# Mixture of experts in a decoder kernel: features on partitions, static order, the expert's weights copied by two engines

## The reference, cut to what matters

```python
logits = x @ gate_w.T + gate_b
topk_logits, topk_idx = jax.lax.top_k(logits, K)          # K = 4
topk_weight = jax.nn.softmax(topk_logits, axis=-1)
xt, gid = xs[order], flat_idx[order]                      # token copies, sorted by expert
gate = jax.lax.ragged_dot(xt, w_gate, group_sizes) + b_gate[gid]
up = jax.lax.ragged_dot(xt, w_up, group_sizes) + b_up[gid]
gate = jnp.minimum(gate, 7.0)
up = jnp.clip(up, -7.0, 7.0)
activated = (up + 1.0) * gate * jax.nn.sigmoid(1.702 * gate)
outs = jax.lax.ragged_dot(activated, w_down, group_sizes) + b_down[gid]
y = jnp.sum(outs[inv].reshape(-1, K, Hh) * topk_weight[..., None], axis=1)
```

## Time and profile before

| | before |
|---|---|
| median of 3 runs | 1018.72 us (1017.98 to 1022.2) |
| the profiled execution's own time | 1018.88 us |
| its span | 1017.2 us |
| TensorE's mean granted clock | 0.884 |
| PE busy | 809.6 us, 80% |
| DVE, ACT, POOL busy | 749.9, 488.3, 459.5 us |
| blocks of experts, first PE instruction to last copy | from 456.15 to 595.2 us of the span |

### The profile page before, as it was taken

The page is one execution under the profiler, slowest core; times in us unless marked ns, Lnnn a source line. Parts: engine busy times, 40 slices in busy tenths (PEclk is TensorE's granted clock), DMA queues, the critical chain, the costliest instruction groups (busy, mean ns, idle before and its releaser), DMA issues. The chain is left out here.

```text
span 1017.2 us, 16391 instructions
## 1 busy us (share of the span) xinstructions
PE 809.6 (80%) x4620; PEld 608.5 (60%) x4624; DVE 749.9 (74%) x1562; ACT 488.3 (48%) x1262; POOL 459.5 (45%) x512
## 2 busy tenths in 40 slices
PE   6798999999799999429999933577799999980165
PEld 3477999997699998317777721224455555550133
DVE  2576777777688887585666635787799999959977
ACT  0233444444355555003333312258898878608185
POOL 1004444442455553536555537140588889813111
PEclk9879999999999999558999975788799999995577
DMA  8707000000400001003444435100333323110000
GB/s 291 245 1 319 14 0 0 0 0 1 174 2 0 0 0 36 6 13 108 125 128 124 124 125 188 60 0 4 124 103 104 99 87 104 42 42 0 0 11 32
DMA packets 29836, 72.06 MB, mean 71 GB/s; under 512 B 5362, under 2 KB 19314, under 8 KB 27298
## 3 DMA queue, kind: packets, MB, share of 16 engines
q1 hardware_dynamic: 25186, 58.95, 16.6%
q0 software_dynamic: 4608, 12.59, 4.7%
HBM read 60.97 MB, written 10.55 MB: 70 GB/s over the span
## 5 line engine op out<-in xcount | busy, mean ns | idle before, releaser
L1718 POOL TENSOR_TENSOR arena<-arena 128x1024 f32<-128x1024 f32 x63 | 147.6, 2371 | 30.7 <-DVE arena L1684 30.7
L1684 DVE TENSOR_TENSOR_SCAN arena<-arena,ps 128x1024 f32<-128x1024 f32 x64 | 143.5, 2275 | 13.6 <-PE ps L1605 8.5
L662 POOL TENSOR_TENSOR arena<-arena 128x256 f32<-128x256 f32 x64 | 46.6, 728 | 195.4 <-DVE arena L656 195.4
L1625 PE MATMUL ps<-arena 128*128 128x512 f32 x256 | 120.1, 592 | 0.0
L712 ACT ACTIVATE arena<-arena 128x128 f32<-128x128 f32 x256 | 98.9, 390 | 19.3 <-DVE arena L682 18.7
L721 ACT ACTIVATE arena<-ps 128x512 f32<-128x512 f32 x64 | 38.2, 598 | 131.4 <-PE ps L609 131.4
L589 PE MATMUL ps<-arena 128*128 (+3 forms) x768 | 96.8, 277 | 2.5 <-PEq L731 0.9
L589 PEld LDWEIGHTS ps<-arena 128*128 128x128 f32 (+1 forms) x768 | 91.5, 193 | 4.1 <-issue 2.9
L1650 ACT ACTIVATE arena<-arena 128x1016 f32<-128x1016 f32 x64 | 72.4, 1135 | 22.9 <-DVE arena L1684 22.8
L1660 ACT ACTIVATE arena<-arena 128x256 f32<-128x256 f32 x192 | 81.2, 494 | 0.1
L1060 POOL DMA_INDIRECT arena<-tokens,arena x64 | 64.0, 1000 | 28.8 <-issue 23.4
(11 more groups left out here) (319 smaller groups left out, 1786.0 us busy)
## 6 DMA issues: line engine op xcount, KB each, us to landing
arena<-c_rows SPq DMA_DIRECT2D x32, 512.0 KB, 3.7
arena<-in_E_gu SPq DMA_DIRECT2D x8, 1024.0 KB, 12.1
expert_out<-arena SPq DMA_DIRECT2D x64, 128.0 KB
arena<-in_E_dn SPq DMA_DIRECT2D x1, 4096.0 KB, 13.7
arena<-in_ctxT SPq DMA_DIRECT2D x2, 1024.0 KB, 5.2
arena<-in_X_o SPq DMA_DIRECT2D x1, 2048.0 KB, 19.9
arena<-in_A_o SPq DMA_DIRECT2D x1, 2048.0 KB, 27.2
arena<-in_F_w SPq DMA_DIRECT2D x2, 1024.0 KB
```

Source lines behind the costliest of these rows:

```text
L1625: t = eng.matmul(ps[:, 2 * k + half, :], ident, hC[s % 4][:, half * 512:(half + 1) * 512], start=False, stop=n == ST - 1)
L1684: eng.tensor_tensor_scan(hst[s % 4], dA[s % 4], psD[s % 2].rearrange("p k m -> p (k m)"), 0.0, ALU.mult, ALU.add).then_inc(h_ready, 1)
L1718: eng.tensor_tensor(hC[s % 4], hst[s % 4], Csb[i % 4], ALU.mult).then_inc(hC_ready, 1)
```

## The change

The steps keep features on partitions throughout, and every engine's order is written out without a loop.

- **Gate and up** (`gate_up`): the weights are now stationary and the turned tokens move. Output is features x tokens, so the activation comes out as the down product needs it: `TA`, `AT`, `actT` are gone. Four fp32 matmuls of 128 columns take the place of two of 256.
- **The weights** of a block must lie at a fixed address for this: `wcur`, two buffers. DVE copies the gate half (`weights`), ACT the up half (`up_weights`), 128x256 fp32 each, at an address from a register that each loads itself (`reg_load`). The copy of block s waits for gate and up of s-2.
- **Biases** of gate and up are now one value for each partition and are added by DVE in the operations that limit (`limits`), again at a register's address; both bias matmuls and `split3` are gone. The down bias, weighted by the gate weights, is added once at the end: before the blocks DVE spreads `gw` over the experts (`prod`, `spread`, operations of 128x1024), PE turns it (two transposes), ACT copies it to `weightT`; after the blocks PE makes eight products of 32 rows and 256 columns, and DVE adds them to `x` in four operations of 128x512 ahead of the combination.
- **Order.** PE: turn of s+2, gate and up of s+1, down of s-1. ACT: up weights of s+2, tokens of s+2, output copy of s-1 (which was DVE's `YO`), sigmoid of s+1. DVE: gate weights of s+2, limits of s+1, gated product of s. POOL gathers directly with `tok_i`, without the copy.
- One more small load (`E_bias_dn`) and a smaller `E_bias`.

```diff
-                    eng.tensor_copy(tok_u[:, v:v + 1], tok_i[:, bass.ds(s + 1, 1)]).then_inc(tok_ready, 1)
                     eng.indirect_dma_start(xin[:, u], None, hd,
-                                           bass.IndirectOffsetOnAxis(ap=tok_u[:, u:u + 1].bitcast(u32), axis=0)
+                                           bass.IndirectOffsetOnAxis(ap=tok_i[:, s:s + 1].bitcast(u32), axis=0)
                                            ).then_inc(x_in[u], 16)
...
-                    for c in range(DC):
-                        eng.matmul(ps[:, 2 + d, 0:2 * I], xinT[:, d, c, :],
-                                   wgu[:, c, bass.ds(e, 1), :].rearrange("p a m -> p (a m)"), start=c == 0, stop=False)
-                    eng.matmul(ps[:, 2 + d, 0:2 * I], sel[0:3 * E, bass.ds(e, 1), :].rearrange("p a m -> p (a m)"),
-                               bias_b[0:3 * E, 0:2 * I], start=False, stop=True).then_inc(gu_done, 1)
-
-                def TA(i, u):
...
-                    eng.transpose(ps[:, 4 + d, 0:P], act_[:, d], ident).then_inc(aT_done, 1)
...
+                def gate_up(s):
+                    d = s % 2
                     eng.wait_ge(xT_ready, s + 1)
+                    eng.wait_ge(wg_ready, s + 1)
+                    eng.wait_ge(wu_ready, s + 1)
+                    if s >= 2:
                         eng.wait_ge(up_ready, s - 1)
+                    for k in range(2):
+                        for c in range(DC):
+                            t = eng.matmul(ps[:, 2 + d, k * I:(k + 1) * I], wcur[:, d, c, k * I:(k + 1) * I],
+                                           xinT[:, d, c, :], start=c == 0, stop=c == DC - 1)
+                    t.then_inc(gu_done, 1)
...
+                def down(s):
...
                     eng.wait_ge(act_ready, s + 1)
...
+                    eng.matmul(ps[:, 6 + d, 0:D], act_[:, d], wdn[:, bass.ds(e, 1), :].rearrange("p a m -> p (a m)"),
+                               start=True, stop=True).then_inc(dn_done, 1)
...
+                for s in range(NBLK + 1):
+                    if s + 2 < NBLK:
+                        turn(s + 2)
+                    if s + 1 < NBLK:
+                        gate_up(s + 1)
+                    if s >= 1:
+                        down(s - 1)
+                    if s < NBLK:
+                        eng.reg_mov(e_down, e_next)
+                    if s + 1 < NBLK:
+                        eng.reg_load(e_next, owner_i[0:1, s + 1:s + 2])
...
+                def up_weights(s):
+                    eng.reg_load(e_a, owner_i[0:1, s:s + 1])
+                    if s >= 2:
+                        eng.wait_ge(gu_done, s - 1)
+                    e = eng.snap(e_a, min_val=0, max_val=E - 1)
+                    eng.activation(wcur[:, s % 2, :, I:2 * I],
+                                   wgu[:, :, bass.ds(e, 1), I:2 * I].rearrange("p c a m -> p c (a m)"),
+                                   ACT.Copy).then_inc(wu_ready, 1)
...
+                for s in range(NBLK + 1):
+                    if s + 2 < NBLK:
+                        up_weights(s + 2)
+                        tokens(s + 2)
+                    if s >= 1:
+                        rows(s - 1)
+                    if s + 1 < NBLK:
+                        sigmoid(s + 1)
...
+                def weights(s):
+                    eng.reg_load(e_w[s % 3], owner_i[0:1, s:s + 1])
+                    if s >= 2:
+                        eng.wait_ge(gu_done, s - 1)
+                    eng.tensor_copy(wcur[:, s % 2, :, 0:I],
+                                    wgu[:, :, bass.ds(owner_of(s), 1), 0:I].rearrange("p c a m -> p c (a m)")
+                                    ).then_inc(wg_ready, 1)
+
+                def limits(s):
...
+                    eng.tensor_scalar(gate[:, d], ps[:, 2 + d, 0:I], bias_gu[:, bass.ds(e, 1), 0], 7.0, ALU.add,
+                                      ALU.min).then_inc(gate_ready, 1)
+                    eng.tensor_scalar(up[:, d], ps[:, 2 + d, I:2 * I], bias_gu[:, bass.ds(e, 1), 1], 8.0, ALU.add,
+                                      ALU.min).then_inc(up_ready, 1)
...
+                for s in range(NBLK):
+                    if s + 2 < NBLK:
+                        weights(s + 2)
+                    if s + 1 < NBLK:
+                        limits(s + 1)
+                    gated(s)
...
+                for b in range(NB):
+                    rows = slice((b % 4) * E, (b % 4 + 1) * E)
+                    t = eng.matmul(ps[:, b, 0:D], weightT[rows, b // 4], bias_dn[rows],
+                                   start=True, stop=True)
...
+                for k in range(NB // 2):
+                    eng.wait_ge(bias_done, k + 1)
+                    two = x[:, 2 * k:2 * k + 2]
+                    ch.mark(eng.tensor_tensor(two, two, ps[:, 2 * k:2 * k + 2, 0:D], ALU.add))
+                ch.wait()
```

More of the change, by code:

```diff
@@ L818, in decoder @@
         sel = view(51104, 2048, "p (e m) -> p e m", dt=bf16, e=E)
-        bias_f = view(A0 + 10240, 512)
-        bias_b = view(A0 + 10752, 256, dt=bf16)
+        bias_gu = view(A0 + 10240, 2 * E, "p (e k) -> p e k", k=2)
+        bias_dn = view(A0 + 10304, D)
+        weightT = view(A0 + 10560, 256, "p (g t) -> p g t", g=2)
         def prefetch_down(eng):
             load(eng, "wdn", wdn, a["E_dn"])
-            load(eng, "bias", bias_f[0:3 * E, :], a["E_bias"])
+            load(eng, "bias", bias_gu, a["E_bias"])
+            load(eng, "bias_dn", bias_dn, a["E_bias_dn"])
             for b in range(NB):
@@ L1079, in _, with turn @@
             def _(eng):
[L1080 to L1085, removed]
+                def turn(s):
+                    d, u = s % 2, s % 4
+                    eng.wait_ge(x_in[u], 16 * (s // 4) + 16)
+                    if s >= 2:
                         eng.wait_ge(xT_ready, s - 1)
@@ new lines, in _ @@
+                loaded(eng, "wgu", "wdn")
+                eng.reg_load(e_next, owner_i[0:1, 0:1])
+                eng.wait_ge(spread_step, 2)
+                for g in range(2):
+                    t = eng.transpose(ps[:, 4, g * P:(g + 1) * P],
+                                      spread[:, 4 * g:4 * g + 4].rearrange("p b e -> p (b e)"), ident)
+                t.then_inc(wT_done, 1)
+                turn(0)
+                turn(1)
+                gate_up(0)
+                for s in range(NBLK + 1):
[9 more added lines that the diff above has]
+                        eng.reg_load(e_next, owner_i[0:1, s + 1:s + 2])
@@ L1141, in _, with tokens @@
             @block.scalar
             def _(eng):
-                def XT(i, u):
-                    s, d = 4 * i + u, u % 2
+                def tokens(s):
+                    d = s % 2
                     eng.wait_ge(xT_done, s + 1)
-                    if not early(i, 2, s):
+                    if s >= 2:
                         eng.wait_ge(gu_done, s - 1)
@@ L1149, in XT, with sigmoid @@
                                    ACT.Copy).then_inc(xT_ready, 1)
-                def SG(i, u):
-                    s, d = 4 * i + u, u % 2
+                def sigmoid(s):
+                    d = s % 2
                     eng.wait_ge(gate_ready, s + 1)
-                    if not early(i, 2, s):
+                    if s >= 2:
                         eng.wait_ge(gs_ready, s - 1)
                     eng.activation(sig[:, d], gate[:, d], ACT.Sigmoid, scale=1.702).then_inc(sig_ready, 1)
[L1158 to L1163, removed]
@@ L1165, in _, with rows @@
-                pipeline(eng, NBLK // 4, [(2, XT), (1, SG), (0, AT)], [(0, XT), (1, XT), (0, SG)], [])
+                def rows(s):
+                    u = s % 4
+                    eng.wait_ge(dn_done, s + 1)
+                    if s >= 4:
+                        eng.wait_ge(y_out[u], 16 * (s // 4))
+                    eng.activation(yout[:, u], ps[:, 6 + s % 2, 0:D], ACT.Copy).then_inc(y_ready, 1)
+                e_a = eng.alloc_register("e_a")
+                def up_weights(s):
+                    eng.reg_load(e_a, owner_i[0:1, s:s + 1])
+                    if s >= 2:
+                        eng.wait_ge(gu_done, s - 1)
[3 more added lines that the diff above has]
+                                   ACT.Copy).then_inc(wu_ready, 1)
@@ new lines, in _ @@
+                loaded(eng, "wgu")
+                up_weights(0)
+                eng.wait_ge(wT_done, 1)
+                eng.activation(weightT, ps[:, 4, 0:2 * P].rearrange("p (g t) -> p g t", g=2), ACT.Copy).then_inc(wT_ready, 1)
+                tokens(0)
+                up_weights(1)
+                tokens(1)
+                sigmoid(0)
+                for s in range(NBLK + 1):
[6 more added lines that the diff above has]
+                        sigmoid(s + 1)
@@ L1183, in GS, with gated @@
+                def gated(s):
+                    d = s % 2
                     eng.wait_ge(sig_ready, s + 1)
@@ L1185, in GS @@
                     eng.wait_ge(gs_ready, s + 1)
-                    if not early(i, 2, s):
```

(25 more changed lines are left out.)

96 lines of the change are left out of this document (27 added, 69 removed).

## The result

| | before | after |
|---|---|---|
| median | 1019.8 us (1017.98 to 1022.2, 4 runs) | 1002.45 us (1001.38 to 1006.94, 4 runs) |
| ratio | | 0.9834, 95% interval 0.9802 to 0.9867 |
| profiled execution, span | 1018.88, 1017.2 us | 1006.94, 1005.2 us |
| stage of the experts | 149.0 us | 131.5 us |
| one block, mean of 50 | 2.10 us | 1.82 us |

The change brings 17.4 us (1019.8 - 1002.45); 28.5 were forecast (27.5 in the blocks, 1.0 at the start).

The account below looks back on a forecast made before the run. PE was taken to bound the blocks: 2.10 us each falling to 1.67, over 64 blocks, saves 27.5 us; with 1.0 at the start, 1018.9 becomes 990.4 us. The range was 981 to 1007 us.

Parts of the forecast that it names:

- rival 1: ACT's queue becomes the bound through a ring over two blocks: 1.85 us a block, 1002 us; chance 0.22.
- PE's own steps: PE in each block: transposes 0.21, gate and up 0.90, down product 0.43, together 1.54 us without stalls.
- Rival 4: PE's four more weight loads a block aren't hidden, 0.19 each: 2.43 us a block, 1039 us; chance 0.03.
- The stalls: PE's late issue kept per block: 0.06 us ahead of the down product and 0.07 unplaced.
- The loop's cost: PE's sequencer late at the loop's turn: 0.085 and 0.05 us a block, both to go with the loop.
- The step that failed: DVE's work per block summed to 1.59 us with its register load overlapped, 1.88 exposed; 1.59 taken, under PE's 1.67.
- Adding the bias through a pointer I cost at nothing: DVE's limits: two register addresses of 0.055 us lie beside running operations, costing nothing; 0.11 if that cover fails.
- second form: DVE's queue becomes the bound if its register load and address are uncovered: 1.88 us a block; no separate chance given.
- Rival 2: PE's sequencer was the bound and stays it: some 2.1 us a block as before, 1018 us; chance 0.06.
- Rival 3: PE, waiting on ACT in each block, is granted 1.2 GHz in place of 2.4: 1036 to 1081 us; chance 0.07.
- Start: Ahead of the first blocks: earlier gathers against PE's turning of the gate weights, gain 0 to 1.5 us, 1.0 taken.
- End: After the blocks: bias products of 3.4 to 6.9 us and DVE's additions hidden by idle PE and gather wait, costing nothing.

Follow-up runs that it names:

- e5: Kernel after with DVE's gated product of a block put ahead of the next block's limits; 987.54 us, 0.9684 of the kernel before.
- e6: Kernel after with both PE's register load moved into gate and up and DVE's gated product ahead of the next limits; 987.5 us, ratio 0.97.
- e7: Kernel before with the stage of the experts written out straight in place of the hardware loop; 1007.47 us, ratio 0.9888.
- e1: Kernel after with PE's register load moved from behind the down product into the middle of gate and up; 990.76 us, ratio 0.9737.
- e8: Kernel after with no register load in PE, the down product using a fixed expert's weights; 995.27 us, ratio 0.9764.
- e4: Kernel after with DVE's two limits taking a fixed expert's bias, without addresses from a register; 997.23 us, ratio 0.9781.
- e3: Kernel after with ACT copying a fixed expert's up weights, without register load or register address; 1001.08 us, ratio 0.9818.

## Why the prediction came out as it did

The sign and the range were right, the likeliest value 12 us too low (990.4 against 1002.45). 1002 was the time of rival 1, but that rival's mechanism was not what happened.

- **PE's own steps: right.** 1.54 a block was forecast from 0.21, 0.90 and 0.43; e5 and e6 run at 1.54 in steady state. Eight loads and matmuls of 128 columns step 0.11, so weight loads are hidden, as the attention's rows had said. Rival 4 is out. That goes against the line that the prediction took from the section "The mechanism" of the Trainium skill's "TensorE: Matmul & The Clock Gate", on loads that overlap only with another row group. The same section also lets a load go ahead where it targets a background weight buffer, and with that the 0.11 agrees.
- **The stalls: mis-sized in both directions.** 0.13 a block was kept for late issue in straight code. Straight code by itself has at most half of it: e7's block steps 1.85 with all its register addresses, and its mean of 1.90 is 0.06 over the steps. The loop's cost was 0.20 a block in place of 0.135. And the kernel after stalls for 0.28 a block (1.82 - 1.54), for a reason that isn't in the sum.
- **The step that failed** is DVE's: its load was summed (1.59 to 1.88 a block) and declared covered, and the ring was drawn for ACT alone. The ring that binds goes through DVE and PE: limits and gated product in DVE's order, down product, PE's register load behind it, transposes, gate and up. Priced from rows it would have been 0.21 + 0.21 + 0.40 + 0.29 on DVE, 0.30 and 0.055 on PE, 0.21 and 0.90 plus hand-overs, some 2.9 us for two blocks, 1.45, and would have been dismissed. The measured ring is 3.63. Four terms were larger: limits with a pointer step 0.27, the load lasts 0.49, the address of the first limit comes after the wait, and gate and up count 1.12 from first start to last end, not the 0.90 of their steps. DVE's list alone was mis-sized as well: 1.59 was taken, on the ground that the load lies beside the last product, and e1 and e8 run at 1.67 and 1.69, because from the start of that product to the copy it is 0.50 and not 0.29.
- **"Adding the bias through a pointer I cost at nothing"**: e4 says 3 to 5 us. The cover named, running operations, isn't there for the first operation behind a wait.
- **Rival 1: its time hit, its mechanism wrong.** e3 takes 0.34 us a block from ACT and nothing changes; that 1002 came out is luck. Its second form, DVE's list at 1.88, was nearer: the list is 1.67, and it is the floor only once PE's load is out of the ring. Rival 2 is out by e5: PE issues a block in 1.54. Rival 3 is out: the clock is 1.00 in every window of 20 us from 480 to 580.
- **Start:** +1.0 was forecast; from the token table to gate and up of block 0 it was 7.9 us (before, 450.55 to 458.49) and is 7.4 (455.72 to 463.12), 0.5 gained.
- **End:** costed at nothing, and it is nothing. The product of the biases took 2.09 us, not 6.9.

The account of the stage, from one profile of each kernel: the loop gone, 11.3 us (e7). From there to the kernel after, 137.6 to 131.5, the new orientation brings 6.1 of the 22.0 that it brings with e5's order (137.6 to e5's 115.6).

A version that beats both kernels is e5: one line moved, 987.5 us, 3.2% under the kernel before.

## What to carry to other kernels

When work is handed round between engines, follow each ring through every engine's program order, register loads and addresses included, and divide by the blocks that it spans; a table of busy shares, or a check that each engine's sum is below the bound, doesn't find it. When one ring is opened, look for the next bound before forecasting its whole price as a gain: here DVE's list stood 0.15 us a block under the ring. In an engine's list put first what is ready (here the gated product of the last block) and last what waits for the newest result. An operation whose address comes from a register pays for the address after its wait, so such an operand is best kept out of the first operation behind a critical wait.

## What was not expected of the hardware

- Eight fp32 products of 32 rows and 256 columns, 16 instructions that each last 629 ns at a granted clock of 0.50, took 2.09 us together, so 0.10 from start to start ((2.09 - 0.63) / 15); full-height ones of 256 columns step 0.43 at the same clock ((1.91 - 0.63) / 3) and 0.215 at full clock. They use the four quarters of rows in turn. The Trainium skill's page "TensorEngine Tiling (Array Packing)", section "Key Properties", says that different tiles of the array can load weights and multiply in parallel; no run here varied the row quarters, so that this is the cause is argued, not shown.
- One and the same register load on PE's sequencer lasted 0.49 us at the median when it stood behind a down product that had just been released, 0.30 when the sequencer ran ahead (e5), 0.28 and 0.30 on ACT and DVE.
- A limit of 128 columns from PSUM steps 0.27 and lasts 0.35 with the bias as a pointer, where it stepped 0.21 and lasted 0.28 to 0.29 with constants alone. In e4, whose pointer has a fixed address, it still lasts 0.35, so the address isn't the cause.
